# The first layer's preparation: zero rows under the spreads, filled waits, later activation tables, four PSUM banks; GpSimd's order at the first level

## The reference

```python
mixed_qkv = hidden_states @ W_qkv                 # 128 -> 2048 columns
beta = jax.nn.sigmoid(hidden_states @ W_b)
g = -jnp.exp(A_log) * jax.nn.softplus(hidden_states @ W_a + dt_bias)
mixed_qkv = _causal_conv_silu(mixed_qkv, conv_w)  # 4 taps over time, then silu
q, k, v = jnp.split(mixed_qkv, [K_DIM, 2 * K_DIM], axis=-1)
q = _l2norm(q) * DK ** (-0.5)
k = _l2norm(k)
# per token, per head:
S = S * jnp.exp(g_t)
kv = jnp.einsum('bhk,bhkv->bhv', k_t, S)
S = S + jnp.einsum('bhk,bhv->bhkv', k_t, (v_t - kv) * b_t)
o_t = jnp.einsum('bhk,bhkv->bhv', q_t, S)
# then norm, gate silu(z), and the output projection
```

## Time and profile before

| | us |
|---|---|
| median of 3 runs (lowest, highest) | 4723.59 (4719.43, 4734.4) |
| the profiled execution | 4747.6 |
| its span, first to last instruction | 4745.9 |
| TensorE busy / weight loads | 4029.2 / 2457.0 |
| VectorE / ScalarE / GpSimd busy | 2463.7 / 1541.4 / 822.1 |

### The profile page before, as it was taken

The page is one execution under the profiler, slowest core; times in us unless marked ns, Lnnn a source line. Parts: engine busy times, 40 slices in busy tenths (PEclk is TensorE's granted clock), DMA queues, the critical chain, the costliest instruction groups (busy, mean ns, idle before and its releaser), DMA issues. The chain is left out here.

```text
span 4745.9 us, 96485 instructions
## 1 busy us (share of the span) xinstructions
PE 4029.2 (85%) x38268; PEld 2457.0 (52%) x38268; DVE 2463.7 (52%) x6106; ACT 1541.4 (32%) x3476; POOL 822.1 (17%) x1452
## 2 busy tenths in 40 slices
PE   6998787898799878789879977878887997787888
PEld 3883343465488334346548833434654883343465
DVE  4674534454567453445456744335545674434553
ACT  3452222341345222234134422223413442222431
POOL 1430000130153000013014300011301430001120
PEclk7998999999799899999979998999997998899999
DMA  2001000000000100000000010000000001000000
GB/s 80 3 3 43 15 18 18 22 36 25 25 3 3 51 7 18 18 22 36 25 25 3 3 57 1 18 18 22 35 25 25 3 8 52 8 11 18 23 35 27
DMA packets 11005, 105.56 MB, mean 22 GB/s; under 512 B 1148, under 2 KB 5552, under 8 KB 6192
## 3 DMA queue, kind: packets, MB, share of 16 engines
q1 hardware_dynamic: 10544, 99.21, 5.4%
HBM read 98.16 MB, written 1.05 MB: 21 GB/s over the span
## 5 line engine op out<-in xcount | busy, mean ns | idle before, releaser
L88 PE MATMUL psum<-ident_bf 128*128 128x512 bf16 x1784 | 515.5, 428 | 204.2 <-DVE l_attn_peak L770 66.6
L88 PEld LDWEIGHTS psum<-ident_bf 128*128 128x128 bf16 x1784 | 178.2, 108 | 465.3 <-issue 172.9
L3044 DVE TENSOR_TENSOR l_attn_xx<-l_attn_xx,psum 128x256 f32<-128x256 f32 x512 | 204.6, 419 | 207.4 <-PE psum L2649 195.6
L2811 ACT ACTIVATE l_attn_ax<-psum 128x128 f32<-128x128 f32 (+1 forms) x768 | 184.9, 279 | 366.1 <-PE psum L2630 251.4
L399 DVE TENSOR_TENSOR l_ffn_hidden<-l_ffn_silu,psum 128x512 f32<-128x512 f32 (+2 forms) x184 | 126.3, 686 | 325.3 <-ACT l_ffn_silu L340 325.1
L94 PEld LDWEIGHTS psum<-streamed_weights,l_ffn_hidden 128*128 128x128 f32 (+2 forms) x1728 | 226.0, 192 | 113.3 <-issue 99.8
L340 ACT ACTIVATE l_ffn_silu<-psum 128x512 f32<-128x512 f32 (+2 forms) x216 | 128.9, 597 | 475.9 <-PE psum L310 475.9
L2645 PE MATMUL psum<-l_attn_ax,l_attn_xx 64*64 64x64 f32 x5120 | 265.0, 222 | 0.0
L2649 PE MATMUL psum<-l_attn_xx,l_attn_ax 64*64 64x64 f32 x5120 | 258.2, 219 | 0.0
L770 DVE TENSOR_REDUCE l_attn_peak<-psum 128x4 f32<-128x2048 f32 (+3 forms) x128 | 185.9, 1487 | 126.2 <-PE psum L688 125.4
L2938 POOL TENSOR_TENSOR l_attn_part<-l_attn_ab,streamed_weights 128x128 f32<-128x128 f32 x640 | 243.3, 413 | 20.3 <-PE psum L2630 20.3
(11 more groups left out here) (522 smaller groups left out, 8141.6 us busy)
## 6 DMA issues: line engine op xcount, KB each, us to landing
streamed_weights<-pack_l_ffn SPq DMA_DIRECT2D x4, 5412.0 KB, 15.4
streamed_weights<-pack_l_ffn SPq DMA_DIRECT2D x4, 3972.0 KB, 13.3
streamed_weights<-pack_l_attn SPq DMA_DIRECT2D x5, 2848.5 KB, 9.4
streamed_weights<-pack_l_xattn SPq DMA_DIRECT2D x4, 2496.0 KB, 8.7
streamed_weights<-pack_l_ffn SPq DMA_DIRECT2D x4, 2192.0 KB, 8.0
streamed_weights<-pack_l_xattn SPq DMA_DIRECT2D x4, 2048.0 KB, 7.4
streamed_weights<-pack_l_ffn SPq DMA_DIRECT2D x4, 1923.0 KB, 8.0
streamed_weights<-pack_l_attn SPq DMA_DIRECT2D x4, 1107.5 KB, 4.9
```

The source lines that it names most:

```text
L88: pe.matmul(self.bank(bank), self.ident_bf[:, :], self.ident_bf[:, :].unsqueeze(1).to_broadcast([P, NT, P]), start=True, stop=True)
L2811: act.activation(ax[b, p, :, :], m.psum[b, p, 0:P].rearrange("p (i t) -> p i t", i=2), ACT.Copy).then_inc(ax_ready, 1)
L3044: dve.tensor_tensor(both, both, m.psum[:, p, P:384], ALU.subtract).then_inc(x_less, 1)
```

## The change

- The `spread` weights get 112 zero rows, and `rsT` becomes [128, 512] with zeros under its 16 rows: GpSimd clears it at the block's start (semaphore `rsT_cleared`, waited for by ScalarE). The spreads are then matmuls over 128 rows.
- Chunks 0 to 7 go to four PSUM banks in turn, those behind to two. TensorE multiplies chunks 0 to 3 without a wait, then issues four fillers; chunk n waits for chunk n - 4 instead of n - 2, up to chunk 9. The norms come one chunk later.
- New fillers: eight ahead of TensorE's wait for the roots, six ahead of chunk 12.
- Exp and Ln move from chunk 1 to chunk 11 on ScalarE, ahead of the copy of `rsT`; the end of g moves from chunk 2 to chunk 13 on VectorE.
- In the recursion GpSimd makes the parts of the first step's first level first, then the sums of the next step, the parts of the second level, and only then the masks of step 0.

```diff
--- before.py
+++ after.py
@@ -2225,6 +2225,7 @@
     NEWTON = 10
     TURNED = [("v", i) for i in range(7)] + [("k", f) for f in range(F)] + [("v", 7)]
     SPREAD_BANKS = (4, 5, 7)
+    chunk_bank = lambda n: n % 4 if n < 8 else n % 2
     with ExitStack() as ctx:
         sb = lambda n, shape, dt=F32: ctx.enter_context(nc.sbuf_tensor(f"{name}_{n}", shape, dt))
         sem = lambda n: m.sem(f"{name}_{n}")
@@ -2250,7 +2251,7 @@
         norm2 = psb("norm2", [P, NT, HV])
         rs = psb("rs", [P, NT, HV])
         rs_tmp = psb("rs_tmp", [P, NT, HV])
-        rsT = psb("rsT", [HV, T])
+        rsT = psb("rsT", [P, T])
 
         in_psum = sem("in_psum")
         tap_ready = sem("tap")
@@ -2264,6 +2265,7 @@
         rs_ready = sem("rs")
         rs_turned = sem("rs_turned")
         rsT_ready = sem("rsT")
+        rsT_cleared = sem("rsT_cleared")
         rs_spread = sem("rs_spread")
         qk_ready = sem("qk")
         gates_psum = sem("gates_psum")
@@ -2315,17 +2317,20 @@
                               start=True, stop=True).then_inc(rs_spread, 1)
 
                 for n in range(C):
-                    if n >= 2:
-                        if n <= NEWTON:
-                            m.warm(pe, 4, 7)
-                        pe.wait_ge(conv_ready, n - 1)
-                    pe.matmul(m.bank(n % 2), w["qkv"][:, ORDER[n], :], m.xnT[:, :], start=True,
+                    if n >= 4:
+                        if n <= NEWTON + 2 and n != NEWTON + 1:
+                            m.warm(pe, 4 if n <= NEWTON else 6, 7)
+                        pe.wait_ge(conv_ready, n - 3 if n < 10 else n - 1)
+                    pe.matmul(m.bank(chunk_bank(n)), w["qkv"][:, ORDER[n], :], m.xnT[:, :], start=True,
                               stop=True).then_inc(in_psum, 1)
-                    if 2 <= n < 10:
-                        norms(n - 2)
+                    if n == 3:
+                        m.warm(pe, 4, 7)
+                    if 3 <= n < 11:
+                        norms(n - 3)
                     if n >= 10:
                         turn("v", n - 10)
                     if n == NEWTON + 1:
+                        m.warm(pe, 8, 7)
                         pe.wait_ge(rs_ready, 1)
                         for t in range(NT):
                             ins = pe.transpose(m.psum[0:HV, 6, tok(t)], rs[:, t, :], m.ident)
@@ -2362,14 +2367,14 @@
                         act.wait_ge(in_psum, n + 1)
                         if n >= 2:
                             act.wait_ge(silu_ready, n - 1)
-                        act.activation(conv[:, n % 2, :], m.bank(n % 2), ACT.Copy,
+                        act.activation(conv[:, n % 2, :], m.bank(chunk_bank(n)), ACT.Copy,
                                        scale=w["conv_w"][:, ORDER[n], 3:4]).then_inc(tap_ready, 1)
-                    if n == 1:
+                    if n == NEWTON + 1:
                         act.activation(a_exp[:, :], w["a_log"], ACT.Exp)
                         act.activation(g_log[:, :, :], g_log[:, :, :], ACT.Ln).then_inc(logged, 1)
-                    if n == NEWTON + 1:
                         act.wait_ge(rs_turned, 1)
-                        act.activation(rsT[:, :], m.psum[0:HV, 6, :], ACT.Copy).then_inc(rsT_ready, 1)
+                        act.wait_ge(rsT_cleared, 1)
+                        act.activation(rsT[0:HV, :], m.psum[0:HV, 6, :], ACT.Copy).then_inc(rsT_ready, 1)
                     if 1 <= n < C + 1:
                         c = ORDER[n - 1]
                         act.wait_ge(conv_ready, n)
@@ -2385,6 +2390,7 @@
 
             @block.gpsimd
             def _(pool):
+                pool.memset(rsT[:, :], 0.0).then_inc(rsT_cleared, 1)
                 for i in range(2 * F):
                     c = ORDER[i]
                     pool.wait_ge(silu_ready, i + 1)
@@ -2420,7 +2426,7 @@
                     dve.wait_ge(tap_ready, n + 1)
                     for i in (2, 1, 0):
                         later = conv[:, n % 2, 3 - i:T]
-                        ins = dve.scalar_tensor_tensor(out=later, in0=m.psum[:, n % 2, 0:T - 3 + i],
+                        ins = dve.scalar_tensor_tensor(out=later, in0=m.psum[:, chunk_bank(n), 0:T - 3 + i],
                                                        scalar=w["conv_w"][:, ORDER[n], i:i + 1], in1=later,
                                                        op0=ALU.mult, op1=ALU.add)
                         if i > 0:
@@ -2428,7 +2434,7 @@
                     ins.then_inc(conv_ready, 1)
                     for i in {12: (0, 1), 13: (2,), 14: (3, 4), 15: (5, 6, 7)}.get(n, ()):
                         normalise(i)
-                    if n == 2:
+                    if n == NEWTON + 3:
                         dve.wait_ge(logged, 1)
                         chain.link(dve.scalar_tensor_tensor(out=g[:, :, :], in0=g_raw[:, :, :], scalar=0.0,
                                                             in1=g_log[:, :, :], op0=ALU.max, op1=ALU.subtract))
@@ -2924,9 +2930,6 @@
 
                 for pairs in (FIRST, SECOND):
                     sums(0, pairs)
-                for pairs in (FIRST, SECOND):
-                    mask(0, pairs)
-                sums(1, FIRST)
                 for n in range(STEPS):
                     for l in range(1, L + 1):
                         for p in range(4 if l < L else 0):
@@ -2937,6 +2940,11 @@
                                 pool.wait_ge(ax_psum, at_part(q - 2, p))
                             pool.tensor_tensor(part[:, q % 2, p, :, :], ab[:, n % 2, p, :, 0:W],
                                                over_block(w["levels"][:, l, :]), ALU.mult).then_inc(part_ready, 1)
+                        if n == 0 and l == 1:
+                            sums(1, FIRST)
+                        if n == 0 and l == 2:
+                            mask(0, FIRST)
+                            mask(0, SECOND)
                         if l == 1 and n >= 2:
                             squares(n - 2)
                         if l == 2 and n + 1 < STEPS:
@@ -3492,7 +3500,7 @@
     return [("qkv", g("W_qkv").reshape(P, 16, P)), ("z", g("W_z")), ("ba", np.concatenate([g("W_b"), g("W_a")], axis=1)),
             ("dt_bias", rep(g("dt_bias"))), ("a_log", rep(g("A_log"))), ("conv_w", tiles_of(g("conv_w"))),
             ("norm_w", np.tile(g("norm_w"), 2)[:, None]), ("out", tiles_of(g("W_out"))),
-            ("levels", np.concatenate([const["levels"][:64, :6, :64]] * 2)), ("ident_blocks", np.tile(np.eye(64, dtype=np.float32), (2, 1))), ("spread", const["spread16"])]
+            ("levels", np.concatenate([const["levels"][:64, :6, :64]] * 2)), ("ident_blocks", np.tile(np.eye(64, dtype=np.float32), (2, 1))), ("spread", np.concatenate([const["spread16"], np.zeros((P - 16, 8, P), np.float32)]))]
```

## The result

The changed kernel takes 4649.9 us (median of 4 runs, 4646.3 to 4655.2), the kernel before 4729.0 beside it (4 runs, 4719.4 to 4741.1). The ratio is 0.9825, with a 95% interval of 0.9812 to 0.9838: 79 us or 1.75% less, where 75 were forecast.

What follows compares the result with a forecast made beforehand. TensorE at half clock was taken to set the pace in the first layer's preparation, with VectorE as floor. Gains 44 - 7 + 32 + 6 = 75 us from the median 4723.6 gave 4649, range 4622 to 4692.

Steps and rivals of the forecast that it cites:

- Part 1: First layer's start, first chunk work to the roots: four banks and later tables gain 44 us, less 7 lost.
- term for slow steps: Behind the first norms: two passes lose two steps at 1.2 GHz, 3.5 us each, 7 us; bounds 0 and 35.
- extra microsecond: Start of pass 1: first two chunks at 1.2 GHz, so roots at 25.8 instead of 24.6 us.
- Part 2: Roots to the next block's memset: 30.8 us against 40.0, 40.0, 35.6, 40.0, with spreads at 2.4 GHz; gain 32 us.
- tail at half clock: Last spread to last copy before the next block: clock expected to fall there in part, 2.0 us added a pass.
- Part 3: Next block's first product: GpSimd's parts first remove a wait, 1.4 us four times, 5.6 us; bounds 0 and 6.
- warm case of part 2: Roots to the next block's memset without the 2.0 us added for the tail: 28.8 us.
- Rows don't count: Clock follows only how busy TensorE is; zero rows do nothing, roots to next block stays 40.0: 4683 us, chance 0.11.
- Recovering clock: Clock falls at the roots or tail but recovers; roots to next block takes 35.6 us: 4668 us, chance 0.17.
- Holds everywhere: Clock never falls: no loss before the roots and a warm tail, gain 90: 4634 us, chance 0.10.
- Slower: Clock falls before the first norms and stays down to the roots, at 42.4 us; rows don't count: 4748 us, chance 0.03.
- does nothing: TensorE isn't the pace after all, so the change makes no difference: 4724 us, chance 0.04.

Runs made afterwards that it cites:

- e11: The kernel before, unchanged, profiled once more beside the other runs and used as second base: 4728.6 us.
- e5: The changed kernel with Exp and Ln back behind the copy of chunk 1 on ScalarE: 4669.0 us, ratio 0.9865.
- e6: The changed kernel with two banks, the old waits and norms for chunks 0 to 9, and no four fillers behind chunk 3: 4676.1 us, ratio 0.9886.
- e2: The kernel before with nothing but the 128-row spreads added: 4709.9 us, ratio 0.9958.
- e9: The changed kernel with added fillers in the recursion, between the turns ahead of the first step and in its last level: 4618.8 us, ratio 0.976.
- e7: The changed kernel with GpSimd's old order in the recursion, masks and sums first: 4653.9 us, ratio 0.9834.
- e1: The changed kernel with the spreads back at 16 rows and no clearing of rsT: 4676.9 us, ratio 0.9887.
- e4: The kernel before, unchanged, run for a second profile: 4736.7 us against 4731.0, ratio 1.0005.

## Why the prediction was right, and where errors cancelled

**Part 1: the gain of 44 was right, the loss of 7 too large.** Against e11 the stretch gained 41.9, against the first profile 43.4, with 24.67 in three passes (24.6 forecast) and 26.34 in pass 3. The clock fell at the first norms in one pass of four and cost 1.7 us, not in two at 3.5. Wrong was the term for slow steps: when it fell, the fillers brought it back within a step. Pass 1 didn't need its extra microsecond. e5 and e6 confirm the two mechanisms: with the early tables the wait is 4.34 again, and with two banks VectorE waits for chunks.

**Part 2: the gain of 32 was too small, mostly by one term.** 30.8 us were forecast and 27.88 measured. The 2.0 added for a tail at half clock were wrong; the other 0.9 is VectorE's work ahead of the tail, whose last chunk ended 21.3 us behind the roots' start and not at 22.3. The clock stayed at 1.00 through the tail in all four passes, though TensorE was busy 0.66 of 2 us there. The first spread at +8.64 (8.9 forecast) and an idle time of 0.70 (1.1) were near. The Silu load takes 1.28 us and Silu starts 1.29 behind it (62.12, 63.41), the price taken from the earlier trace rows. The Trainium skill, "ScalarE: Activation LUTs", section "What ACT_TABLE_LOAD costs", adds a drain to each switch for 2.66 us in all; between 62.12 and 63.41 there is no room for one.

**Part 3: 2.1 us a pass, 8.3 in all, for 5.6 forecast.** The part came in time, as said, and that removed the wait of 1.50. Of the 0.64 that remain, 0.2 is the clock, which was down over the last turns in before and up in three of four passes after. Another 0.2 is that the product starts before the last turn has ended, as the rows show it, when it needn't wait. The last 0.2 is that this turn starts earlier: ahead of it VectorE's L2986 took 0.73 us in before, beside GpSimd's mask of 0.74, and the same instruction (now L2994) takes 0.50 after, beside a part of 0.52. The forecast counted the idle time alone.

**Not in the prediction: 8 us given back** in a level that nothing in the change touches. The step that failed is the silence in the sum about code behind the change. A cover that was 0.5 busy held its clock in before, and I took that for granted.

**Sum.** Against the run that lies at the median: 41.9 + 37.3 + 8.3 - 8.2 = 79.3, and 78.6 by the layer's own length. Forecast 44 - 7 + 32 + 6 = 75. Two terms on the clock were too pessimistic (5 in part 1, 8 in the tail), the warm case of part 2 and part 3 were short by 4 and 3, the give-back of 8 was missing, and the gains were counted from a profile in which the first stretch was 1 us and the second 7 us longer than in e11. These errors cancel; a forecast within a microsecond of the median is luck in that.

**The rivals.** "Rows don't count" (4683) is refuted by e2. "Recovering clock" (4668): the stretch was 27.9 in all passes, not 35.6. "Holds everywhere" (4634) was the right picture of this block in three passes of four. Of the 16 us between its price and the result, 8 are the give-back in the next block and 5 the base (4729.0 for 4723.6). e9, in which the clock holds there too, came out below 4634. "Slower" fell with the clock of 1.00 behind the first norms, "does nothing" with the result. (Its roots at 42.4 would be 5.4 to 7.3 us later than before, not 6.5 to 7.3, and its time about 4746; this changes nothing here.)

**What stays open.** Why the same half-busy level keeps its clock in some passes and loses it in others is not shown. e2 has the instructions of before from the memset on and loses it in all four passes; e7 has before's order and loses it too. But two passes of changed kernels keep it: pass 3 of the kernel after and pass 1 of e6, e1 loses it in two passes whose block began at 1.2 GHz, and before keeps it though its clock is back a microsecond ahead of the memset. So neither the instructions nor the clock at the block's start decide. There are 44 passes in the eleven profiles without fillers there, and one thing read from the granted clock separates them: the moment of the earlier fall, the one at the block's start. In the 14 passes that keep the clock it began 3.2 to 3.8 us ahead of the first product (the 12 of before) or at it (within 0.1 us, the other two). In the 30 that lose it, it began 4.4 or 1.7 to 2.5 us ahead of the first product, or 0.3 to 1.0 behind it. Within one kernel 0.3 us decide: e6 keeps it in pass 1 (fall at 0.0) and loses it in pass 3 (fall at 0.3). So the fall in the level goes with a small shift in time, which makes it unlikely that the work done long before decides it; no run shifts that moment alone, so this is a correlation and not a shown cause. e9 removes the fall, it doesn't explain it.

## What to carry to other kernels

Where the trace shows TensorE busy throughout and the granted clock at one half, check how many rows its matmuls use: padding 16 rows with zeros to 128 cost 0.52 us on an idle engine and nothing on TensorE, and turned a stretch of 33 to 40 us into one of 29. Then read the granted clock of the stages behind the change as well, since a clock won in one place can be lost in the next thin stretch (2 to 3 us a pass here), and put fillers into its gaps even when these are below half a microsecond. Before pricing a stretch whose clock is unsteady, take a second profile of the unchanged kernel; ours differed by 10 us in one layer.

## What the runs showed of the hardware that was not expected

- Rows full of zeros count for the granted clock. TensorE busy without a break with 16-row spreads was at 0.50 (3.00 of 3.00 us, before); with 128 rows, of which 112 are zeros, at 1.00. 64 rows did little better than 16 in the same stretch (30.9 against 30.9 to 31.3 us, 27.9 for 128).
- Few rows don't always cost the clock: 16-row spreads kept a clock of 1.00 that they found (e1, 72 to 74), and in 5 of 12 passes (before, e4, e11) won back one that was lost, after 10 to 14 us at 0.50. In e2, with 128 rows, it was back after 7 us in all four passes.
- Work about half busy in gaps of 0.37 us can hold 1.00 (before, 146 to 147) or fall to 0.50 (after, 119 to 122), even in two passes of one kernel (after, pass 3 and pass 1).
- The clock's return varies from execution to execution in mid-kernel: one stretch of one unchanged kernel took 40.0, 33.3 or 35.6 us. The Trainium skill, "TensorE: Matmul & The Clock Gate", section "What's actually happening", says for a kernel's start that the number of slow matmuls differs between runs of the same kernel; what it says of the start these passes show in mid-kernel.
- VectorE's L2986, 128x128 in SBUF, took 0.73 us beside GpSimd's mask of 0.74 (before) and 0.50 beside a part of 0.52 (after, L2994), ending 0.15 us behind GpSimd's instruction both times, and 0.28 where GpSimd did nothing.
